# Stacking the three bf16 parts of dt*u in rows, so that one matmul per scan group selects and adds them

## The reference, cut to what matters

```python
dt  = jax.nn.softplus(dbc[..., :DT_RANK] @ dt_proj_w.T + dt_proj_b)     # [b, l, 128]
dA  = jnp.exp(dt[..., None] * A)                                        # [b, l, 128, 16]
dBu = dt[..., None] * Bm[:, :, None, :] * xs[..., None]                 # dt * u * B
_, hs = jax.lax.associative_scan(combine, (dA, dBu), axis=1)            # h = dA * h + dBu
y = jnp.einsum('blds,bls->bld', hs, Cm) + xs * Dvec
```

## Time and profile before

| | |
|---|---|
| median of 3 runs | 5355.45 us (5351.28 to 5372.19) |
| the profiled execution | 5343.31 us, its span 5341.4 us |
| PE busy | 4435.6 us, 83% of the span |
| DVE busy | 4141.3 us, 78% |
| POOL busy | 3949.6 us, 74% |
| ACT busy | 3305.9 us, 62% |
| DMA | 623.36 MB, 255561 packets, 117 GB/s |
| `pick_du` matmuls (L686) | 5376, in 1792 slots |

### The profile page before, as it was taken

How to read it: one execution, slowest core, us unless ns; L and a number is a source line. 1 busy time by engine, 2 the same in 40 slices (tenths; PEclk the granted TensorE clock), 3 DMA queues, 4 the chain that set the end, 5 groups by cost and what they waited for, 6 DMA issues and landing times. The chain is left out here.

```text
span 5341.4 us, 71012 instructions
## 1 busy us (share of the span) xinstructions
PE 4435.6 (83%) x21206; PEld 1807.8 (34%) x21206; DVE 4141.3 (78%) x6297; ACT 3305.9 (62%) x5293; POOL 3949.6 (74%) x4937
## 2 busy tenths in 40 slices
PE   3577788888888888888888888788888888888887
PEld 1223333333333333333333333333333333332332
DVE  2278888788878887888878888788878888788871
ACT  1255466666666666666666666666666667666665
POOL 1267787778877877887878788778777778788872
PEclk9588899999999998999999999899999999999997
DMA  2365655555545554555555555455555555454420
GB/s 69 69 140 140 139 131 116 126 123 129 123 118 128 124 130 108 132 132 122 128 117 133 123 126 127 112 122 127 121 115 125 130 120 131 112 118 112 97 67 5
DMA packets 255561, 623.36 MB, mean 117 GB/s; under 512 B 105268, under 2 KB 170676, under 8 KB 255028
## 3 DMA queue, kind: packets, MB, share of 16 engines
q1 hardware_dynamic: 255156, 618.60, 50.2%
HBM read 540.85 MB, written 77.65 MB: 116 GB/s over the span
## 5 line engine op out<-in xcount | busy, mean ns | idle before, releaser
L1184 POOL TENSOR_TENSOR hc<-hs,cb 128x448 f32<-128x448 f32 x1792 | 2045.7, 1144 | 839.1 <-DVE hs L1021 810.3
L1021 DVE TENSOR_TENSOR_SCAN hs<-dtb,state,ps 128x448 f32<-128x448 f32 x1792 | 2049.0, 1143 | 110.2 <-DVE ps L1011 3.4
L1011 DVE TENSOR_TENSOR ps<-ps,bb 128x448 f32<-128x448 f32 x1792 | 1099.4, 614 | 508.8 <-PE ps L686 507.5
L686 PE MATMUL ps<-dux,pick 128*128 128x448 bf16 x3584 | 1066.3, 380 | 162.0 <-DVE hs L1021 99.7
L864 ACT ACTIVATE dtb<-dtb,decay 128x448 f32<-128x448 f32 x1792 | 1091.3, 658 | 95.7 <-DMA dtb<-dt_scratch 94.1
L906 ACT ACTIVATE hg<-ps,be 128x448 f32<-128x448 f32 x896 | 520.1, 631 | 576.9 <-PE ps L750 576.7
L686 PE MATMUL ps<-duz,pick 128*128 128x448 bf16 x1792 | 660.5, 369 | 0.0
L750 PE MATMUL ps<-xn,we 64*128 64x448 f32 x1792 | 578.2, 619 | 45.1 <-ACT hg L906 43.6
L895 ACT ACTIVATE rz<-ps,bnb 128x448 f32<-128x448 f32 x448 | 281.3, 628 | 476.3 <-DVE yw L1108 256.7
L686 PEld LDWEIGHTS ps<-dux,pick 128*128 128x128 bf16 x3584 | 273.1, 101 | 862.2 <-issue 444.3
L733 PE MATMUL ps<-h,w 96*128 96x448 bf16 x896 | 313.7, 385 | 219.6 <-ACT rz L895 82.3
(11 more groups left out here) (177 smaller groups left out, 6426.5 us busy)
## 6 DMA issues: line engine op xcount, KB each, us to landing
dtb<-dt_scratch SPq DMA_DIRECT2D x448, 896.0 KB, 6.6
slab<-h_scratch SPq DMA_DIRECT2D x168, 290.0 KB, 8.1
dt_scratch<-sp SPq DMA_DIRECT2D x112, 224.0 KB, 2.0
h_scratch<-h2p SPq DMA_DIRECT2D x168, 112.0 KB
h<-h_scratch SPq DMA_DIRECT2D x56, 336.0 KB, 4.2
h_scratch<-h1s SPq DMA_DIRECT2D x56, 232.0 KB, 3.7
xw<-xn_scratch SPq DMA_DIRECT2D x112, 112.8 KB, 2.7
xw<-xn_scratch SPq DMA_DIRECT2D x112, 112.5 KB, 2.7
```

Of the source, the lines that this page charges most:

```text
L686: last = MM(ps[BU[n % 3]][:, 0:CH], pick[:, i, :], part, start=(a == 0), stop=(a == 2))
L1011: V.tensor_tensor(bank, bank, bb[:, k % 2, :], ALU.mult).then_inc(bu_ok, 1)
L1021: V.tensor_tensor_scan(rev(hs[:, n % RH, :], d), rev(dtb[i // 4][:, i % 4, :], d), rev(bank, d), state[:, d, i:i + 1], ALU.mult, ALU.add). ...
L1184: P_.tensor_tensor(hc[:, n % 8, :], hs[:, n % RH, :], cb[:, k % 2, :], ALU.mult).then_inc(hc_ok, 1)
```

## The change: three parts in rows 0 to 95 of one tile

The inner channels stand in four blocks of 32 rows, and slot i takes its channels from block i // 4. After the change a tile `du3[:, k % 2, j, :]` holds in rows 0 to 31 the first part of block j, in rows 32 to 63 the second, in rows 64 to 95 the third, and zeros below. A matmul adds over rows, so one of 128 rows both picks and adds. `pick` becomes four matrices instead of sixteen.

DMAs move the rows: for each part four DMAs of 32 rows by 448 bf16 (28 KB each), from `dup` to `du3`, so 12 in a step, issued by SP. The parts are now made in another way: ACT rounds to bf16 (`round_du`, two in a step), and POOL subtracts. So POOL's three steps of `part` stand in slots 3, 6 and 9, with ACT's in its slots 7 and 10, and the softplus is put one slot earlier. SP's three `stack_du` stand in slots 8, 10 and 11.

```diff
-        pick = sb("pick", [128, DS, 128], BF16)
+        pick = sb("pick", [128, 4, 128], BF16)
-        dux = sb("dux", [128, 2, 2, CH])
-        duz = sb("duz", [128, 2, CH], BF16)
+        dux = sb("dux", [128, CH])
+        dup = sb("dup", [128, 3, CH], BF16)
+        du3 = sb("du3", [128, 2, 4, CH], BF16)
...
+                    def stack_du(kk, a):                              # SP
+                        if a < 2:
+                            sp_.wait_ge(da_ok, 2 * n2(kk) + a + 1)
+                        else:
+                            sp_.wait_ge(dx_ok, 3 * n2(kk) + 3)
+                        if run and kk >= 2:
+                            sp_.wait_ge(bu_ps, DS * (kk - 1))
+                        for j in range(4):
+                            sp_.dma_start(du3[32 * a:32 * a + 32, kk % 2, j, :], dup[32 * j:32 * j + 32, a, :])\
+                               .then_inc(du_in[kk % 2], 16)
...
+                                if i == (8, 10, 11)[j] and second_half(k):
+                                    stack_du(k + 1, j)
...
                     def pick_du(n):                                   # PE
                         k, i = n // DS, n % DS
                         if i == 0 and k:
-                            pe.wait_ge(dx_ok, 3 * k)
+                            pe.wait_ge(du_in[k % 2], 192 * ((k - 1) // 2 + 1))
                         if n >= 3:
                             pe.wait_ge(h_ok, n - 2)
-                        for a in range(3):
-                            part = duz[:, k % 2, :] if a == 2 else top(dux[:, k % 2, a, :])
-                            last = MM(ps[BU[n % 3]][:, 0:CH], pick[:, i, :], part, start=(a == 0), stop=(a == 2))
-                        last.then_inc(bu_ps, 1)
+                        MM(ps[BU[n % 3]][:, 0:CH], pick[:, i % 4, :], du3[:, k % 2, i // 4, :], start=True, stop=True)\
+                            .then_inc(bu_ps, 1)
...
+                    def round_du(kk, a):                              # ACT
+                        act.wait_ge(dx_ok, 3 * n2(kk) + a + 1)
+                        if a == 0 and n2(kk):
+                            act.wait_ge(du_in[(kk - 1) % 2], 192 * (n2(kk - 1) // 2 + 1))
+                        A.activation(dup[:, a, :], dux[:, :], ACT.Copy).then_inc(da_ok, 1)
...
+                            if i in (7, 10) and second_half(k):
+                                round_du(k + 1, (7, 10).index(i))
...
                     def part(kk, a):                                  # POOL
-                        x = dux[:, kk % 2]
                         if a == 0:
                             pool.wait_ge(dt_ok, n2(kk) + 1)
-                            if run and kk >= 2:
-                                pool.wait_ge(bu_ps, DS * (kk - 1))
-                            P_.tensor_tensor(x[:, 0, :], sp[:, 1, :], u[:, kk % 2, :], ALU.mult).then_inc(dx_ok, 1)
+                            P_.tensor_tensor(dux[:, :], sp[:, 1, :], u[:, kk % 2, :], ALU.mult).then_inc(dx_ok, 1)
                         else:
-                            pool.wait_ge(dx_ok, 3 * n2(kk) + a)
-                            out = x[:, 1, :] if a == 1 else duz[:, kk % 2, :]
-                            P_.tensor_tensor(out, x[:, a - 1, :], top(x[:, a - 1, :]), ALU.subtract).then_inc(dx_ok, 1)
+                            pool.wait_ge(da_ok, 2 * n2(kk) + a)
+                            if a == 2 and n2(kk):
+                                pool.wait_ge(du_in[(kk - 1) % 2], 192 * (n2(kk - 1) // 2 + 1))
+                            out = dux[:, :] if a == 1 else dup[:, 2, :]
+                            P_.tensor_tensor(out, dux[:, :], dup[:, a - 1, :], ALU.subtract).then_inc(dx_ok, 1)
...
-                            if i in (4, 5, 6):
-                                part(k + 1, i - 4)
+                            if i in (3, 6, 9):
+                                part(k + 1, i // 3 - 1)
```

More of the change, by code:

```diff
@@ L286, in _ @@
                 then(V.tensor_copy(identb[:, :], ident[:, :]))
-                for i in range(DS):
-                    then(V.tensor_copy(pick[:, i, :].rearrange("p (s e) -> p s e", e=8),
-                                       ident[:, :].rearrange("p (j e q) -> p j q e", j=4, q=4)[:, i // 4, i % 4, :]
-                                       .unsqueeze(1).to_broadcast([128, DS, 8])))
+                then(V.memset(pick[96:128, :, :], 0.0))
+                then(V.memset(du3[96:128, :, :, :], 0.0))
+                for q in range(4):
+                    for a in range(3):
+                        lanes = slice(32 * a, 32 * a + 32)
+                        then(V.tensor_copy(pick[lanes, q, :].rearrange("p (s e) -> p s e", e=8),
+                                           ident[lanes, lanes].rearrange("p (e q) -> p q e", q=4)[:, q, :]
+                                           .unsqueeze(1).to_broadcast([32, DS, 8])))
                 for d in range(2):
@@ L377, in build @@
         dtb_in = [sem(f"dtb_in{j}") for j in range(4)]
-        dt_e, dt_l, sp_ch, dt_ok, dx_ok = (sem(n) for n in ("dt_e", "dt_l", "sp_ch", "dt_ok", "dx_ok"))
+        dt_e, dt_l, sp_ch, dt_ok, dx_ok, da_ok = (sem(n) for n in ("dt_e", "dt_l", "sp_ch", "dt_ok", "dx_ok", "da_ok"))
+        du_in = [sem("du_in0"), sem("du_in1")]
         bu_ps, bu_ok, a_ok, h_ok, st_ok, hc_ok, y_acc, gated, o_ps, o_rd, st0 = (sem(n) for n in
@@ L405, in rev @@
             return ap[:, ::-1] if d else ap
-        def top(ap):
-            return ap.bitcast(BF16)[:, 1::2]
         def emit(p, run, a_imgs, e_imgs):
@@ L668, in _ @@
                             sp_.wait_ge(dtb_in[j], 16 * (n2(STEPS) + 1))
+                        sp_.wait_ge(du_in[STEPS % 2], 192 * (n2(STEPS) // 2 + 1))
                 @block.tensor
@@ L1293, in _ @@
                                 soft_le(k + 1)
+                                soft_ym(k + 1)
                             if i == 1:
[L1295 removed]
+                                soft_log(k + 1)
                             if i == 2:
[L1297 to L1298 removed]
                                 soft_dt(k + 1)
[L1300 to L1301 removed]
+                            if i in (3, 6, 9):
+                                part(k + 1, i // 3 - 1)
                         for a in (1, 2):
```

3 lines of the change are left out of this document (removed).

## The result

The changed kernel takes 5547.16 us (median of four runs, 5536.99 to 5554.85) against 5358.64 for the kernel before, a ratio of 1.0344 with a 95% interval of 1.0319 to 1.037. Forecast were 5105 us, with a chance of 0.11 for slower. Rows and counts come from one profiled execution of each kernel. Its clock can differ a little from the median of all runs of the kernel, and where runs are compared by their clock the medians are given.

A forecast was written before the change was run, and what follows sets the result against it. The prediction took DVE and PE taking turns as the bound; 260 us gained less 15 for ACT's roundings gave 245 us less, 5098 us from the profiled 5343, stated as a median of 5105 us, range 4950 to 5275 us.

The forecast's parts named there:

- The bound (DVE and PE take turns): In a step neither DVE nor PE fills the time; each waits for the other, DVE 507.5 us for the pick.
- What the two matmuls give: Two of three matmuls gone from each pick: 0.40 us of PE a slot, and 260 us less time in all.
- The 3.0 us of the even step: Gain taken for an even step: half of DVE's 6.04 us of waiting for PE, ten picks being worth 4.0 us.
- the clock: PE's mean granted clock, 0.922 before, was expected at about 0.90, between 0.89 and 0.91.
- the 260 us: The gain taken for the whole kernel from DVE waiting less for PE, between estimates of 235 and 300 us.
- The sign that the prediction named for this: The forecast is wrong if DVE's waits for PE stay over 550 us in sum.
- The third rival: PE pauses more often and its clock falls more often: 5400 us, slower; chance 0.08.
- its argument against itself: One pick in place of three makes the lower clock level cheaper, below the priced 0.56 us for each us.
- POOL's reordering at nothing: POOL's same instructions in another order, with two waits for ACT, cost nothing, hidden behind up to six slots of lead.
- ACT's wait: ACT's first rounding waits about 3 us for POOL's first part in odd steps, 0.3 us uncovered; 15 us in all.
- DMAs and the stacked tile: Twelve more DMAs a step, 2.3 us per group of four, landing 2.0 us; tile whole in time, nothing added.
- The sum: Whole kernel: 260 less 15, so 245 us less; 5098 us from the profiled 5343, given as 5105 for a median.

The follow-up runs named there:

- e16: The kernel before with five zero matmuls ahead of the transposes of the next image's tokens in slot 14; 0.9858, -76 us.
- e8: The kernel before with two of its three matmuls in each pick, the third part made but not added; 0.9961, -21 us.
- e13: The kernel before with one matmul in each pick, plus zero matmuls in PE's two pauses (slot 5 of even steps, slot 14); 0.9938.
- e2: The kernel before with only the first of its three matmuls in each pick, the other parts made but not added; 1.0019, +10 us.
- e14: The kernel before with zero matmuls in two pauses of PE: five in slot 14, four in slot 5 of even steps; 0.9836, 5268.17 us.
- e18: e16 with its five zero matmuls behind the transposes of slot 14 in place of ahead of them; 0.998, -11 us.
- e17: The changed kernel with the zero matmuls of e14 in PE's two pauses; 1.0221, 5471.35 us.
- e3: The changed kernel with the whole new chain (softplus, POOL's parts, ACT's roundings, SP's DMAs) one slot later; 1.0117, +63 us.
- e7: The changed kernel with only POOL's second part moved, from slot 6 to slot 7; 1.0269, +144 us.
- e12: e2 plus ACT's two roundings in slots 8 and 11, into a tile that nobody reads; 1.0061.
- e11: e2 plus the twelve DMAs of a step in slots 9, 11 and 12, into a tile that nobody reads; 1.0024.
- e1: The changed kernel with its one pick matmul issued three times on the same operands; 1.0259, +139 us.
- e5: e2 plus two zero-weight matmuls ahead of PE's wait for the scan in slots 10 to 15 and 0 to 3; 1.024.
- e9: e5 with the identity as the weights of the filling matmuls in place of zeros; 1.024.
- e15: e3 with the zero matmuls of e14 in PE's two pauses; 1.0039.

## Why the prediction was wrong

*The bound (DVE and PE take turns): right.* Nothing in the runs speaks against it, and e16 shows it from the other side: with fewer falls PE is faster and the time shorter.

*What the two matmuls give: right at full clock in the odd step.* The walk gave 1.2 us for an odd step with both; e8 has 0.51 to 0.73 us for one, e13 1.3 and 1.5 us for both. The 3.0 us of the even step, half of the 6.04 us of waiting by choice, weren't measured: neither e8 nor e2 has an even step without a fall in images 2 to 7.

*Failed step: the clock.* The forecast took the 260 us as kept and the mean clock at 0.89 to 0.91. It was 0.843 in e2, with nothing changed but the matmuls: 765 us more at the lower level than before (medians), and all of the gain gone (+10 us in place of -260). The sign that the prediction named for this came in the changed kernel, DVE's waits for PE over 550 us in sum (754). The third rival had named the clock, with a break-even at a mean clock of 0.88 and a chance of 0.08, and its argument against itself, that one pick makes the lower level cheaper, holds too: e2 breaks about even at 0.843, so if the 260 us are right the price there was near 270 / 765 = 0.35 us for each, not 0.56 (an estimate). What was missed is that PE saves its time just where it waits next. Where the rows show it, what is saved lengthens the pause ahead of DVE's scan (1.02 to 1.44 us), or the one ahead of ACT's result is longer too (1.86 before, 2.63 in e2), and where such a pause stands ahead of heavy work, that work runs at half the clock (`down` 1.72 to 3.26 us). The rows for it stood in the trace of before: in the even step of the earlier trace rows, pauses of 1.86 and 1.87 us ahead of the falls at 2567.49 and 2591.38; e16 and e14, with the pauses filled, and e18, with the same work elsewhere, show that such pauses cause falls. That the longer pauses of the changed kernel cause its falls too is shown by e17 for two places; for the others it is inferred from the rows.

The Trainium skill's page "TensorE: Matmul & The Clock Gate", section "A second HAM failure mode: psum-queue depth-cycling", has it that a PE that idles briefly between groups of matmuls swings between its two clocks and loses throughput. The rival by that rule had 0.08 and was the right one: the trace agrees, with 131 falls before and 224 in e2.

*Failed step: POOL's reordering at nothing.* The walk asked only whether a result comes late. It comes in time; but the second part stands between two `by_c` in the slot where DVE normalises, and DVE's work grew by 119 us. The slot as a whole cost 121 of the 184 us (e3); that some 95 of them are DVE's longer work is an estimate from e7.

*ACT's wait: right in the odd step, unseen elsewhere.* The rounding of the step looked at, with the burst behind it:

```profile
2711.27 0.58 ACT L952 ACTIVATE dup<-dux 128x448 bf16<-128x448 f32 x1 [3.51 <-POOL dux L1234]
2711.87 1.28 ACT L921 ACT_TABLE_LOAD   x1
2713.16 1.16 ACT L921 ACTIVATE hg<-ps,be 128x448 f32<-128x448 f32 x2
```

It waits 3.51 us, and the table load is over at 2713.15, about when PE's first four matmuls of the burst are (the pick behind them starts at 2712.89). Forecast was a wait of 3 us and 0.3 uncovered. But 93 steps of 112 have such a wait and not 56, and the roundings themselves cost 23 us (e12) where 15 stood for all.

*DMAs and the stacked tile: right.* Forecast were 2.3 us for four issues and a landing of 2.0. The page's row, and SP's timeline:

```profile
du<-dup SPq DMA_DIRECT2D x1344, 28.0 KB, 2.8
```

```profile
2684.19 2.43 SPq L563 DMA_DIRECT2D du<-dup  x4
```

The last group of this step, issued until 2686.62, has landed at about 2689.4 by the median of 2.8, and the next step begins at 2699.15. The forecast's own sum, 2627 + 2.3 + 2.0, is 2631.3 and not 2631.5, which changes nothing. No wait for it is among the larger ones, and e11 prices the twelve at 3 us.

*The sum.* Forecast -260 + 15 = -245. (5098 + 12 is 5110 us; the recorded 5105 is 5 us off, which doesn't matter here.) Measured: the matmuls +10 (e2), the roundings +23 (e12), the DMAs +3 (e11), not taken apart +27 (to e3), the slot too early +121 (e3), together +184.

## What to carry to other kernels

An engine that works in turns with others may not keep the time that it saves; it waits longer, and for PE a longer pause ahead of heavy work can cost as much as was saved, as in e2. So before taking matmuls out of a kernel at a high granted clock, list PE's pauses next to its falls, and try filling a pause with zero matmuls first: here that gave 88 us, where taking two matmuls out of each pick gave nothing. When work on POOL is moved, look at what DVE does on SBUF alone in that slot, not only at who waits for the result.

## What the runs showed of the hardware

- Kernels that differ only in the number of bf16 matmuls of a pick, three, two or one, had clocks of 0.914, 0.890 and 0.843 (medians of all runs). The changed kernel had 0.830, and 0.921 with its matmul issued three times on the same operands (e1).
- Matmuls with zero weights had the same clock and time as with the identity (e5 and e9: 0.863 and 0.862 by the medians, both 1.024).
- A DVE operation with two inputs in SBUF took 0.42 us beside one short POOL instruction and 2.79 us beside an unbroken row of POOL's, while DVE's scan, which reads one of its inputs from PSUM, took 1143 ns in the mean before and after. The `pwd` operation of 112x4 elements went from 201 to 646 ns in the mean.
- Where pauses were filled, each us less at the lower clock gave 0.34 us in e16 (76 of 224), 0.27 in e14 (88 of 321), 0.17 in e13 (43 of 253), 0.29 in e15 (42 of 144) and 0.25 in e17 (66 of 267), all by the medians; the profiled executions alone would give from 0.13 to 0.68.
